# Dealing rows out by twos instead of fours: 1 KB pieces in DRAM and a column step of two at the scan

## The reference

```
x = x + 0.5 * ffn(layernorm(x))
x = x + attn(layernorm(x))
x = x + 0.5 * ffn(layernorm(x))

ffn:  e = argmax(x_ @ router.T)                      # 8 experts, one chosen per row
      y  = (silu(x_ @ gate[e].T) * (x_ @ up[e].T)) @ down[e].T
      ys = the same with the shared weights w_gate_s, w_up_s, w_down_s
      return y + ys
attn: bound     = circular_convolution(x, bind_key)
      hologram  = for each of the 16 sequences, h[t] = d * h[t-1] + bound[t], d = sigmoid(decay)
      retrieved = circular_correlation(hologram, unbind_key)
      return x + gate * retrieved
```

## Time and profile before

| | |
|---|---|
| median of 3 runs | 293.8 us (293.01 to 297.62) |
| the profiled execution, its own time | 292.21 us |
| its span in the profile | 290.5 us |
| PE busy, share of the span | 257.8 us, 89% |
| DVE busy | 189.4 us, 65% |
| POOL busy | 179.4 us, 62% |
| DMA moved | 27.51 MB in 24244 packets |

### The profile page before, as it was taken

How to read it: one execution, slowest core, us unless ns; L and a number is a source line. 1 busy time by engine, 2 the same in 40 slices (tenths; PEclk the granted TensorE clock), 3 DMA queues, 4 the chain that set the end, 5 groups by cost and what they waited for, 6 DMA issues and landing times.

```text
span 290.5 us, 6435 instructions
## 1 busy us (share of the span) xinstructions
PE 257.8 (89%) x1788; PEld 215.9 (74%) x1788; DVE 189.4 (65%) x734; ACT 160.3 (55%) x374; POOL 179.4 (62%) x260
## 2 busy tenths in 40 slices
PE   0889999979999999986699999999779999999980
PEld 0547677558999999845577878676469999999560
DVE  4796664954555555448999999676845556655355
ACT  2744353236777777326498877732157777777210
POOL 6646777713777777723457888767505758887700
PEclk9999999999999999997679999899999999999997
DMA  6871111323333321144000101101423433311078
GB/s 210 314 310 40 55 47 60 109 69 80 101 98 107 98 78 38 38 122 172 0 1 23 35 28 38 49 29 56 124 66 88 107 88 105 92 55 48 27 250 329
DMA packets 24244, 27.51 MB, mean 95 GB/s; under 512 B 4967, under 2 KB 17645, under 8 KB 23952
## 3 DMA queue, kind: packets, MB, share of 16 engines
q1 hardware_dynamic: 17648, 16.06, 18.6%
q0 software_dynamic: 4544, 8.54, 9.0%
q10 hardware_dynamic: 2016, 2.50, 2.4%
HBM read 15.37 MB, written 12.62 MB: 96 GB/s over the span
## 4 chain that ended last, share of the span: by engine, by line
PE 45%; POOL 17%; DVE 14%; issue 12%; DMA 4%; ACT 3%; SPq 1%; DVEq 1%; ACTq 0%; POOLq 0%
PE bank L960 13%; PE bank L883 12%; POOL returned L386 10%; PE bank L891 6%; PE bank L968 6%; POOL dispatched L357 3%; DMA xres<-in_x 3%; PE bank L908 3%; PE bank L914 2%; DVE st_f L558 2%; DVE hs L631 2%; DVE xres L599 2%; POOL token L380 1%; PE bank L869 1%; POOL scale_f L346 1%
## 5 line engine op out<-in xcount | busy, mean ns | idle before, releaser
L386 POOL DMA_INDIRECT returned<-ey,token x78 | 76.6, 982 | 32.9 <-issue 18.0
L960 PE MATMUL bank<-xsT,wgu 128*128 128x128 f32 x624 | 82.9, 276 | 2.5 <-DVE xres L599 1.5
L960 PEld LDWEIGHTS bank<-xsT,wgu 128*128 128x128 f32 x624 | 75.7, 192 | 3.7 <-DVE xres L599 1.8
L357 POOL DMA_INDIRECT dispatched<-xn,slot x64 | 63.5, 993 | 23.7 <-issue 17.7
L883 PE MATMUL bank<-xnT,gu 128*128 128x512 f32 x128 | 65.1, 636 | 4.3 <-DVE hs L631 3.5
L813 DVE COPY ey<-bank 128x128 f32<-128x128 f32 x78 | 22.8, 292 | 45.6 <-PE bank L968 45.5
L489 ACT ACTIVATE wgu<-gu 128x512 f32 x78 | 48.2, 623 | 4.1 <-issue 3.9
L462 ACT ACTIVATE sg<-bank 128x512 f32<-128x512 f32 x32 | 18.9, 591 | 54.5 <-PE bank L883 47.1
L968 PE MATMUL bank<-wdn,eh 128*128 128x128 f32 x312 | 47.5, 276 | 0.5 <-DVE eh L808 0.5
L511 ACT ACTIVATE eg<-bank 128x256 f32<-128x256 f32 x78 | 29.9, 384 | 32.6 <-PE bank L960 32.4
L968 PEld LDWEIGHTS bank<-wdn,eh 128*128 128x128 f32 x312 | 40.9, 192 | 0.9 <-DVE eh L808 0.9
(11 more groups left out here) (102 smaller groups left out, 292.9 us busy)
## 6 DMA issues: line engine op xcount, KB each, us to landing
xs<-dispatched SPq DMA_DIRECT2D x80, 66.0 KB, 1.8
ey<-returned SPq DMA_DIRECT2D x16, 256.0 KB, 4.3
gu<-in_gu SPq DMA_DIRECT2D x1, 2048.0 KB, 12.6
out<-xres ACTq DMA_DIRECT2D x8, 256.0 KB, 2.9
returned<-ey,token POOLq DMA_INDIRECT x78
xres<-in_x SPq DMA_DIRECT2D x1, 1024.0 KB, 8.1
dn<-in_dn SPq DMA_DIRECT2D x1, 1024.0 KB, 15.1
dispatched<-xn,slot POOLq DMA_INDIRECT x64
```

The costliest lines, as they stand in the source:

```text
L357: nc.gpsimd.indirect_dma_start(dispatched[:, :], bass.IndirectOffsetOnAxis(slot[:, i:i + 1], 0), xn[:, i, :], None, bounds_check=last_row) ...
L386: nc.gpsimd.indirect_dma_start(returned[:, :], bass.IndirectOffsetOnAxis(token[:, b:b + 1], 0), ey[:, b, :], None, bounds_check=last_back, ...
L960: last = nc.tensor.matmul(bank[4 + b % WR][:, i * P:(i + 1) * P], wgu[:, b % WR, i * P:(i + 1) * P], xsT[:, b // 2 % 2, b % 2, :], start=T ...
```

## The change

Rows are dealt out by twos. A group of 512 rows is now two halves (`PAIR = 2`) of 256 rows, each one sequence; partition p holds rows 2p and 2p+1 of each half. In DRAM a group is 256 pieces of 1 KB, for the four loads of x, the sixteen reads of `returned` and the eight stores. `every_other` takes half h and parity u of the columns, so the transposes at L869 for the scan write every second column of one half of the bank, and the product at L914 reads every second column of one half of `scanned`. Column order within a group is still the order of time. The row numbers that `iota` writes into `xn` follow the new layout. The number of instructions on each engine, their order and their waits are as before, and the tiles that they work on have the same shapes; only the access patterns of the DMAs (128x512 becomes 128x2x256 for one group) and of L869 and L914 differ.

```diff
+PAIR = TPG // 2
-    def by_four(rows):
-        return rows.rearrange("(k p t) c -> p k (t c)", p=P, t=TPG)
-    x_dram, out_dram = (by_four(v.rearrange("b t c -> (b t) c")) for v in (x_in, out))
+    def by_two(rows):
+        return rows.rearrange("(j p t) c -> p j (t c)", p=P, t=2)
+    x_dram, out_dram = (by_two(v.rearrange("b t c -> (b t) c")) for v in (x_in, out))
-    returned_dram = by_four(returned[0:N, :])
+    returned_dram = by_two(returned[0:N, :])
...
         def groups(buf, lo, hi):
-            return buf[:, lo * TPG:hi * TPG, :].rearrange("p (k t) c -> p k (t c)", t=TPG)
+            return buf[:, lo * TPG:hi * TPG, :].rearrange("p (j t) c -> p j (t c)", t=2)
-        def by_row(ap):
-            return ap.rearrange("p (j t) -> p j t", t=TPG)
+        def every_other(ap, t):
+            return ap.rearrange("p (h j u) -> p h u j", h=PAIR, u=2)[:, t // 2, t % 2, :]
...
-                sp.dma_start(groups(xres, lo, hi), x_dram[:, lo:hi, :]).then_inc(x_in[i], 16)
+                sp.dma_start(groups(xres, lo, hi), x_dram[:, lo * PAIR:hi * PAIR, :]).then_inc(x_in[i], 16)
-                    sp.dma_start(groups(back, k, k + 1), returned_dram[:, k:k + 1, :]).then_inc(back_in[k], 16)
+                    sp.dma_start(groups(back, k, k + 1), returned_dram[:, k * PAIR:(k + 1) * PAIR, :]).then_inc(back_in[k], 16)
-            nc.gpsimd.iota(xn[:, :, C].bitcast(I32).rearrange("p (k t) -> p k t", t=TPG), [[GC, G], [1, TPG]], base=0,
-                           channel_multiplier=TPG, **small).then_inc(const_made, 1)
+            nc.gpsimd.iota(xn[:, :, C].bitcast(I32).rearrange("p (j t) -> p j t", t=2), [[2 * P, NT // 2], [1, 2]],
+                           base=0, channel_multiplier=2, **small).then_inc(const_made, 1)
-                act.dma_start(out_dram[:, k:k + 1, :], groups(xres, k, k + 1)).then_inc(stored, 16)
+                act.dma_start(out_dram[:, k * PAIR:(k + 1) * PAIR, :], groups(xres, k, k + 1)).then_inc(stored, 16)
...
-                    to = by_row(tp["a"][:])[:, :, t] if kind == "a" else tp["f"][:, t * P:(t + 1) * P]
+                    to = every_other(tp["a"][:], t) if kind == "a" else tp["f"][:, t * P:(t + 1) * P]
                     last = nc.tensor.transpose(to, src[:, at * TPG + t, 0:C], ident[:])
-                        last = nc.tensor.matmul(tp["a"][:, t * C:(t + 1) * C], by_row(scanned[:, q, :])[:, :, t],
+                        last = nc.tensor.matmul(tp["a"][:, t * C:(t + 1) * C], every_other(scanned[:, q, :], t),
                                                 mix[:], start=True, stop=True)
```

## The result

| | before | after |
|---|---|---|
| median, 19 runs each | 293.04 us (291.96 to 297.62) | 296.14 us (293.57 to 299.85) |
| ratio | 1 | 1.0079, 95% interval 1.0053 to 1.0104 |
| the profiled execution, its own time | 292.21 us | 294.75 us |
| its span | 290.5 us | 293.0 us |

The change costs 0.79%, 2.3 us (1.6 to 3.0): little, but the interval leaves out "no change". In the changed kernel a line's number is one higher: L915 is the product behind the scan, L870 the transposes, L961 the experts' first product.

A forecast was written before the change was run, and what follows sets the result against it. DVE sets the pace from 131 to 153 us, PE with POOL beside it up to the second experts, DMA the tail. -1.5 + 0.3 + 0.1 + 1.1 = 0.0 on 292.2, plus 1.3 for the median: 293.5 us (291.0 to 296.5).

The forecast's parts named there:

- The step of two loads as fast as a dense one: Product behind the scan: eight weight loads take 0.97 us instead of 1.94, about 1.0 us less per group (at least 0.65).
- The transposes at nothing: Transposes for the scan, writing every second column: between nothing and 0.05 us a group, counted as nothing.
- Six of the eight give nothing, and PE stands idle in their place: Six of eight L914 runs save nothing, since DVE (to 153 us) and POOL with DVE (153 to 178) keep their pace.
- The fourth rival: PE falls to half clock more often between 153 and 178 us: 295.4 to 296.9 us in all, chance 0.08.
- The middle gives 1.5 us: Seventh and eighth L914 give 1.0 us each, capped by POOL's 1.57 us wait: 1.5 us (1.3 to 1.8).
- 0.3 at most: Half clock behind the seventh L914 may move or vanish, worth 1.6 us on PE; POOL's cap leaves 0.3 at most.
- Everything behind it, the second experts and the tail, moves with it: Second experts and tail start earlier by the middle's 1.5 us, since PE and the read-back start that much earlier.
- The transfers, +1.5 us: 1 KB pieces, taken 10% dearer: +0.3 us at the start, +0.1 first read-back, +1.1 tail.
- forecast 1.1: Tail, where the DMA engines are full for 11 us: 1 KB pieces add 1.1 us (0 to 2.8).
- forecast 0.3: Start, where DVE waits for the last load of x: 1 KB pieces add 0.3 us (0 to 0.7).
- SBUF Cachelines: Skill's rule for L914's loads: step of two free, step of four not; saves 1.0 us per group, straight line 0.65.

The follow-up runs named there:

- after_gap: The changed kernel plus nine extra products of zeros on PE in the waits just ahead of the second experts: 1.0029 of the kernel before.
- cols_gap: The kernel before with only the columns by two (2 KB pieces kept), plus nine extra products ahead of the second experts: 0.9976 of the kernel before.
- before_gap: The kernel before plus the same nine extra products ahead of the second experts, as a control: 1.0006 of the kernel before.
- pieces_only: The changed kernel with 1 KB pieces, but transposes and product take every fourth column as before: 1.0052 of the kernel before.
- best_warm: The changed kernel with 2 KB reads of `returned` and extra products at the start, in the middle and ahead of the second experts: 1.0079 of before.
- x_2kb: The changed kernel with x loaded in 2 KB pieces by fours; read-backs and stores keep 1 KB: 1.0097 of the kernel before.
- cols_only: The kernel before with 2 KB pieces kept, but transposes and product take every second column: 1.0031 of the kernel before.
- returned_2kb: The changed kernel with the sixteen reads of `returned` in 2 KB pieces; x and output stay by twos: 1.0038 of the kernel before.
- tail_1kb_only: The kernel before with only read-backs and stores in 1 KB pieces: 1.0013 of the kernel before.
- x_1kb_only: The kernel before with only the loads of x in 1 KB pieces: 0.9994 of the kernel before.

## Why the prediction failed

- **The step of two loads as fast as a dense one** (L914 loses about 1.0 us per group): right, 0.9 us. The transposes at nothing: right enough; their median went from 326 to 375 ns, perhaps because the low clock covers more of the first stretch (0.61 against 0.70).
- **Six of the eight give nothing, and PE stands idle in their place**: right, 22.60 of 25 us. The clock falls more before 178 us, where PE has room. The fourth rival had this happen without room for it; it didn't decide.
- **"The middle gives 1.5 us", because POOL waits 1.57 us for PE**: this term of the sum failed. That POOL comes in as the next limit was right, but I took its wait for a property of the kernel. It is a wait for the products at the half clock behind the seventh L914, which I priced at "0.3 at most". In three of the five profiles by four that fall and that wait are missing, and the last scatter is as early as with the columns by two. Over fifteen it comes 0.6 us earlier, the start of the second experts 0.5.
- **"Everything behind it, the second experts and the tail, moves with it"**: this step failed too. I wrote that PE could start at 211.9 and the rows would be there at 212.1, with 0.24 us between the chains. I took PE's work at either start to be of one price. But with the columns by two PE arrives first. In four of the six profiles by two without fillers here it waits 2.0 us and more, its clock falls to the half as it starts, and the first 16 records of the experts take 2.9 to 3.6 us in place of 2.0. None of the four by four has this, though two of them waited 1.93 and 2.08 us. With idle products in the wait (`after_gap`, `cols_gap`) the 16 stay at 2.02 us and the stage at 62.7 us; both kernels get 0.5% back, and the kernel before gets nothing (`before_gap`). That the clock costs 1.2 to 1.5 us where it falls is shown. That the gap's fillers win their 0.5% by this alone is not, since fillers elsewhere won as much. How long the wait is hangs also on the scatter's landing, 2.4 or 3.8 to 4.1 us. The late landing of `before_gap` (3.97) did not show in the start of its second experts (149.75, mean 149.62), because its last scatter was early (142.01).
- **The transfers, +1.5 us**: `pieces_only` says 1.5 us (0.7 to 2.3), its two halves apart add up to 0.2 with intervals that allow 1.5, and the profiles say +0.9 in the tail (forecast 1.1) and +0.6 at the start (forecast 0.3), the latter not clear of the scatter. So the term stands, and its tail is right within 0.2 us.
- With these sizes the sum is -0.5 (the start of the second experts, mean of ten profiles, four of them with fillers in the gap) + 1.5 (transfers) + 1.0 (the half clock, up to 1.5 us in four profiles of six) = 2.0 us. Measured are 2.3 (1.6 to 3.0).
- The columns alone, with both kinds of fillers, came to the forecast's 1.5 us (0.9948). The way isn't the forecast one, so the agreement proves little.

Of my theories on the start one stays open: that 1 KB loads cost time because the second run of four shared products is then more often at the half clock. No experiment changed that run alone, and the profiles speak for it weakly (three of eight with 1 KB loads, one of seven with 2 KB). Having the first shared products at the full clock gives nothing (`best_warm` 1.0079). Large pieces for x did not win the start back over the executions: `x_2kb` 1.0097.

The Trainium skill (Advanced Engine Details and Errata, "SBUF Cachelines") holds here in both halves: two hits per line of 16 bytes give loads of 197 ns median where a step of four gave 329.

## What to carry to other kernels

Where two chains meet within a few tenths of a microsecond, shortening one of them makes its engine wait, and on PE that wait can have a price beyond itself: behind waits of 2.0 to 3.4 us, work of 2.0 us took 2.9 to 3.6. Before booking a saving, ask what stands at the meeting point, and put a few idle products there as a test. A wait read from one execution (POOL's 1.57 us) is a sample; ask what caused it, and look for it in several profiles before it caps a sum. Here it came from a clock that had fallen just ahead of it. Small pieces cost where the DMA engines are full: a byte cost 12% more in 1 KB than in 2 KB pieces, and the tail took 0.9 us more.

## What was unexpected in the hardware

- The last indirect scatter (128 rows) landed either in 2.3 to 2.5 us or in 3.8 to 4.1, with nothing between in fifteen profiles. Of the six times that a fetch of instructions fell beside it, five were the long ones.
- The granted clock stayed at 1.00 through PE's waits and fell only 0.2 to 0.9 us after the products behind them had begun (an estimate from short windows of `after`, `cols_only`, `x_2kb` and `returned_2kb`).
- Waits of 1.93 us before the first expert product left the clock up (`tail_1kb_only`: 2.02 us for 16 records), waits of 2.00 did not (after: 3.53), and once 2.08 did (`x_1kb_only`: 2.02): the sum of the waits alone doesn't decide.
- A load of a stationary operand with a step of two in float32 costs about the same as a dense one, 197 ns a record against 192 for the router's, and one with a step of four costs 308 to 332 ns whatever the clock.
